# Wide elementwise operations moved from GpSimd to VectorE, and the routing and hand-over work of attention spread over its tiles, in a three-stage transformer block

## The chip, the cores and the metric

One core of one Trainium2 chip. The metric is device time in microseconds (us) of one execution.

## The reference

x is (4, 1024, 128) in float32: four batches of 1024 rows. Three stages are added onto x in turn.

```python
x = x + 0.5 * ffn(layernorm(x))        # pass 0
x = x + attn(layernorm(x))
x = x + 0.5 * ffn(layernorm(x))        # pass 1, same weights
# ffn(t): logits = t @ Wr.T + br; two best of 8 experts, softmax over the two
#   expert e: relu(t @ W1[e].T + b1[e]) @ W2[e].T + b2[e], hidden size 512
#   returns layernorm(t + weighted sum of the two) * gamma + beta
# attn(t): softmax(q1 k1^T) - lambda * softmax(q2 k2^T), times v, then an rms norm
```

## The kernel before

TensorE is PE, VectorE DVE, ScalarE ACT, GpSimd POOL, SyncE SP. A batch is 8 tiles of 128 rows (TB = 8, BATCHES = 4).

**The two passes.** For each batch the rows t are made by ACT (`make_rows`, L561), turned by PE (`turn_rows`), multiplied into logits (`logits`), and DVE picks the experts (`read_logits`, `choose`) and the place of each row (`place`), with an exponential by ACT (`gap`) and prefix sums by PE (`prefix`) between them. `copy_rows` makes the second copy of the rows and the one in `tgt`. POOL then writes each 128 rows with an indirect DMA to their expert's region in DRAM (`scatter`, L424, 16 pieces for a batch); `table` lists the tiles of the experts for a group of two batches. A pass is 78 slots, one tile of one expert each, 39 for a group. In a slot SP loads the rows (ring of 8), PE turns them (L842), multiplies with W1 (L850) and W2 (L860), ACT and DVE stage weights (L604, L1199) and take the results out of PSUM (L611, L1206, `add_b2` L1214). In pass 0 SP writes the results and POOL gathers them back (`gather`, L435); in pass 1 POOL sends each tile of results away with an indirect DMA (`send`, L446), and SP loads them when a group is through. Each `load` of SP in pass 1 also waits until the `send` of 8 slots earlier has landed, and loads of a group wait until all its rows are written (`group_ready`). Every engine's stream is one fixed order: the loops over slots `s` say in which slot a side job stands (STATS_AT = 1, TURN_AT = 9, CHOOSE_AT = 13, PLACED_AT = 20, GSLOTS = 39, LAST_AT = 45). POOL executes its stream in order, so a job behind a scatter waits for it.

**Merging.** The two results of a row are weighted and added to `tgt`, normalised (DVE statistics, POOL `rstd`: reciprocal root in L407 to L410; ACT `normalise`), multiplied with gamma, and added to x with beta. Before, POOL does the wide parts, each one instruction over a batch, 128 x 1024: `add_beta` (L416), `merge_add` (L462, L465), `add_tokens` (L470), `gain` (L476). Pass 0's batch 0 is merged in the slots of pass 0, batches 1 to 3 in attention, in tiles of the batch ahead. Pass 1 merges in its second half and in the tail after the last slot.

**Attention.** Query tile i of batch b: PE `scores` (L784 to L786) into banks 0 to 3, one pair for each softmax; DVE takes two maxima (L1374), ACT two exponentials (L667), DVE the difference (L1385) one tile later, PE turns the difference of two tiles earlier (`turn`, L910), ACT copies it (L641), and for each half batch PE multiplies with the values (`values`, L921, two pieces of 8 matmuls) and Wv. The next score pair of PE can start only when the exponential of the tile before has read its bank. The order around the change in the streams before: PE in tile i does `scores(i)`, then the extras, then `turn(i-2)`, and `values(b, 0, ·)` in tiles 6 and 7; DVE does the maxima of i, `difference(i-1)`, then the extras: `merge_tiles` in tiles 0 and 1, `add_values` and `x_stats(b-1)` in tile 4, `x_stats(b+1)` in tile 5. POOL in each batch does rstd, `merge_add`, `value_scale`, eight gathers or scatters, and only then the rstd of the two `x_stats`, which ACT's `make_rows` in tile 5 and `make_xn` in tile 6 wait for. At the end of a batch stand `logits`, `choose` and `place` of the batch before, and the hand-over to the next batch: `turn_xn`, `copy_xnT`, `xnT_rest`, `multiply_M`, `copy_xm`, `xm_rest`. `tgtT` lies in the memory of `sum_r`, which the merge of the next batch uses.

The lines that the text names are numbered as in the profile.

## Time and profile before

| | us |
|---|---|
| median of three runs | 785.39 (783.78 to 787.7) |
| the profiled execution, own time | 786.02 |
| its span | 784.3 |
| PE busy in the span | 588.6 (75%) |
| DVE busy | 518.8 (66%) |
| ACT busy | 413.5 (53%) |
| POOL busy | 384.9 (49%) |

The span runs from the first to the last instruction of the profiled execution; its own time has 1.7 us around it. Starts are us from the span's start. Start-up and first routing take the first 88 us, pass 0 then goes to about 251, attention to 549, pass 1 to 745, and the rest is the tail. Busy shares are means over these stages and say little by themselves.

### The profile page before, as it was taken

The page shows a single profiled execution, that of the slowest core. Times are in us where ns is not written, and L with a number is a line of the kernel's source. Part 1 is how long each engine was busy: PE and PEld are TensorE (multiplying, and loading weights), DVE is VectorE, ACT ScalarE, POOL GpSimd, SP SyncE. Part 2 cuts the span into 40 slices and gives each one's busy share as a digit, 9 for nine tenths or more (in the row PEclk, how much of TensorE's full clock was granted, in tenths as well). Part 3 has the DMA queues.
Part 4 walks back from the last instruction along what each step waited for, and adds up shares of the span by engine and source line. Part 5 has one row for each costly group of instructions (what it writes and reads, how often), then busy time and mean ns, then how long its engine had stood idle before and what let it go on. Part 6 is the DMA issues. An engine that isn't in the chain of part 4 may idle for free.

```text
span 784.3 us, 16226 instructions
## 1 busy us (share of the span) xinstructions
PE 588.6 (75%) x3864; PEld 508.4 (65%) x3864; DVE 518.8 (66%) x1630; ACT 413.5 (53%) x1103; POOL 384.9 (49%) x415
## 2 busy tenths in 40 slices
PE   2654599998998678976887667787989858788900
PEld 2544599998988555554655455653988747778900
DVE  4654666675786786994799476853648635888726
ACT  3443266655556377376647644653665434646621
POOL 6455055544453067168157313413556774666643
PEclk9955599999899999998999797998999988999965
DMA  8412244324331001001000001001122321412141
GB/s 281 123 56 62 54 106 109 93 69 111 95 93 52 1 10 41 3 12 34 11 28 21 8 7 49 24 4 47 40 65 72 97 62 47 152 54 59 45 161 54
DMA packets 53677, 49.18 MB, mean 63 GB/s; under 512 B 9863, under 2 KB 45875, under 8 KB 53073
## 3 DMA queue, kind: packets, MB, share of 16 engines
q1 hardware_dynamic: 44736, 31.25, 14.6%
q0 software_dynamic: 8640, 16.87, 7.0%
q8 instruction: 35, 0.57, 0.3%
q14 instruction: 58, 0.47, 0.2%
q10 hardware_dynamic: 208, 0.02, 0.0%
HBM read 25.99 MB, written 23.02 MB: 62 GB/s over the span
## 4 chain that ended last, share of the span: by engine, by line
PE 48%; DVE 20%; issue 11%; POOL 10%; ACT 6%; DMA 3%; DVEq 1%; ACTq 0%; POOLq 0%; SPq 0%
PE banks L850 15%; PE banks L860 14%; PE banks L921 5%; PE banks L828 3%; POOL zb L435 3%; ACT rowbuf L561 2%; PE banks L842 2%; PE banks L819 2%; POOL rs L408 2%; PE banks L784 2%; POOL rows L424 2%; PE banks L786 2%; PE banks L785 2%; DVE nb L1374 1%; DVE sum_r L1241 1%
## 5 line engine op out<-in xcount | busy, mean ns | idle before, releaser
L850 PE MATMUL banks<-scratch 128*128 128x128 f32 x1248 | 174.2, 284 | 19.4 <-DVE scratch L1199 16.8
L850 PEld LDWEIGHTS banks<-scratch 128*128 128x128 f32 x1248 | 157.7, 198 | 27.0 <-issue 20.5
L860 PE MATMUL banks<-blocks,scratch 128*128 x1248 | 169.1, 280 | 0.1
L860 PEld LDWEIGHTS banks<-blocks,scratch 128*128 128x128 f32 x1248 | 156.2, 197 | 0.7 <-issue 0.5
L1206 DVE TENSOR_SCALAR scratch<-banks,blocks 128x128 f32<-128x128 f32 x312 | 95.0, 345 | 65.7 <-PE banks L850 64.5
L424 POOL DMA_INDIRECT rows<-rowbuf,slot x96 | 95.6, 996 | 67.4 <-issue 37.7
L667 ACT ACTIVATE scratch<-banks,nb 128x1024 f32<-128x1024 f32 x64 | 71.1, 1114 | 81.0 <-DVE nb L1374 80.7
L611 ACT ACTIVATE scratch<-banks,blocks 128x128 f32<-128x128 f32 x312 | 97.7, 364 | 28.5 <-PE banks L850 27.6
L598 ACT ACTIVATE scratch<-banks 128x128 f32<-128x128 f32 x156 | 43.2, 277 | 128.7 <-PE banks L842 126.4
L1374 DVE TENSOR_REDUCE nb<-banks 128x1 f32<-128x1024 f32 x64 | 76.8, 1217 | 48.1 <-PE banks L786 47.0
L446 POOL DMA_INDIRECT results<-scratch x78 | 77.7, 996 | 61.0 <-DVE scratch L1214 43.0
L435 POOL DMA_INDIRECT zb<-yrows,slot x64 | 64.8, 1012 | 53.4 <-DVE scratch L1214 25.1
L784 PE MATMUL banks<-xnTh,xmh 128*128 128x512 f32 x128 | 59.8, 467 | 36.2 <-ACT scratch L667 29.8
L1199 DVE COPY scratch<-blocks 128x256 f32 x156 | 63.4, 407 | 27.3 <-PE banks L850 18.7
L1214 DVE TENSOR_TENSOR scratch<-banks,blocks 128x128 f32<-128x128 f32 x156 | 45.0, 289 | 32.6 <-PE banks L860 23.8
L921 PE MATMUL banks<-scratch,xn 128*128 128x512 f32 x128 | 62.6, 637 | 1.5 <-ACT scratch L641 1.5
L604 ACT ACTIVATE scratch<-blocks 128x256 f32 x156 | 63.7, 408 | 0.1
L842 PE MATMUL banks<-ident,scratch 128*128 128x128 f32 x156 | 43.9, 281 | 23.5 <-issue 12.2
L784 PEld LDWEIGHTS banks<-xnTh,xmh 128*128 128x128 f32 x128 | 26.3, 205 | 48.2 <-ACT scratch L667 33.9
L424 POOL DMA_INDIRECT rows<-scratch,slot x32 | 30.5, 953 | 51.9 <-DVE scratch L1214 51.9
L786 PE MATMUL banks<-xnTh,xml 128*128 128x512 f32 x128 | 54.2, 423 | 0.0
L785 PE MATMUL banks<-xnTl,xmh 128*128 128x512 f32 x128 | 53.9, 421 | 0.0
(175 smaller groups left out, 893.0 us busy)
## 6 DMA issues: line engine op xcount, KB each, us to landing
scratch<-rows SPq DMA_DIRECT2D x156, 64.5 KB
yrows<-scratch SPq DMA_DIRECT2D x78, 64.0 KB
scratch<-results SPq DMA_DIRECT2D x3, 1024.0 KB, 7.8
rows<-padrows SPq DMA_DIRECT2D x34, 64.5 KB
x<-in_L_attn_x_dram SPq DMA_DIRECT2D x4, 512.0 KB, 6.0
scratch<-in_L_ffn_W_dram SPq DMA_DIRECT2D x1, 2048.0 KB, 19.2
out_dram<-x SPq DMA_DIRECT2D x4, 512.0 KB, 6.1
rows<-rowbuf,slot POOLq DMA_INDIRECT x96
```

Source lines behind the costliest of these rows:

```text
L424: pool.indirect_dma_start(rows[b // GB], bass.IndirectOffsetOnAxis(slot_v[:, b, j, k:k + 1], 0), rows_of(p, b)[:, j, k, :], None).then_inc ...
L435: pool.indirect_dma_start(zb[:, i * D:(i + 1) * D], None, yrows[b // GB], bass.IndirectOffsetOnAxis(slot[:, b * PAIRS + i:b * PAIRS + i + ...
L446: pool.indirect_dma_start(results, bass.IndirectOffsetOnAxis(xt_v[:, r, D:ROW].bitcast(I32), 0), ys[:, r * D:(r + 1) * D], None, bounds_ch ...
L611: ins = act.activation(hT_of(T, c), hT_at(T, c), ACT.Relu, bias=blocks[:, B1_AT + c:][:, bass.ds(at, 1)], scale=1.0)
L667: act.activation(pp, banks[:, 2 * m * 512:(2 * m + 2) * 512], ACT.Exp, bias=nb[:, 2 * i + m:2 * i + m + 1], scale=1.0, accum_out=ll[:, i:i ...
L784: pe.matmul(o, ah, bh, start=True, stop=False)
L786: return pe.matmul(o, al, bh, start=False, stop=True)
L850: ins = pe.matmul(hT_at(T, c), staged(T, c), xT_of(T), start=True, stop=True)
L860: ins = pe.matmul(y_at(T), hT_of(T, c), blocks[:, W2_AT + c * D:][:, bass.ds(at, D)], start=(c == 0), stop=(c == FC - 1))
L921: ins = pe.matmul(bank(6), xn[b % 2][:, k * D:(k + 1) * D], dT[g][:, k * QG * P:(k + 1) * QG * P], start=(k == 0), stop=(k == TB - 1))
L1206: ins = dve.tensor_scalar(hT_of(T, c), hT_at(T, c), blocks[:, B1_AT + c:][:, bass.ds(at, 1)], 0.0, ALU.add, ALU.max)
L1374: dve.tensor_reduce(nb[:, c], banks[:, 2 * m * 512:(2 * m + 2) * 512], AX_X, ALU.max, negate=True).then_inc(nb_ready, 1)
```

## The change

It does the following.

- POOL's wide operations go to DVE, each in two halves of 128 x 512: beta of pass 0 in slots 18 to 25, beta of pass 1 in slots 31 to 38, the gain and the addition of the merge in attention's tile 5, tokens and gain of pass 1 in slots from LAST_AT + 5 and LAST_AT + 20 on and in the tail.
- In attention POOL does the rstd of both `x_stats` ahead of most gathers and scatters. The scatters of batch 0 stand in batches 2 and 3, those of batch 1 in batch 3; 8 of batch 2's stand ahead of the first send of pass 1, the other 8 one per slot in slots 0 to 7. Those of batch 3 are two per slot, in slots 20 to 27.
- `tgtT` gets a buffer of its own. The routing of batch b-2 (logits, choose, place) moves from the end of batch b-1 into tiles 1 to 3 of batch b (b = 2, 3); only that of batch 2 stays at the end of batch 3. `table(0)` moves into tile 4 of batch 3.
- `make_rows`, `make_xn` and the normalisation of the merge are done in halves in two tiles. `values(b, 0, 1)` and `turn(b, 5)` of PE go ahead of `scores(b, 7)`; `turn_xn` follows it. The waits for the split query matrix go into each score.
- DVE does `xnT_rest` in tile 7 and `xm_rest` ahead of the last difference, `add_values(b, 0)` in tile 0 of the next batch.

The core of the diff:

```diff
-        tgtT = sum_r
+        tgtT = sb("tgtT", S)
+        BETA_AT = 18
+        SENT_BEFORE = 8
+        def halves_of(tiles):
+            return range(tiles * TB // 2, (tiles + 1) * TB // 2)
+        def choose_tile(b):
+            return 1 if b == BATCHES - 1 else 2
...
 POOL, attention
-                if b > 1:
-                    scatter(1, b - 2, range(TB))
-                if b < BATCHES - 1:
-                    rstd(n)
-                    n += 1
-                    merge_add(b + 1)
-                if b:
-                    value_scale(b - 1, 1)
-                if b < 2:
-                    gather(b + 2, range(TB))
-                if b > 1:
-                    scatter(1, b - 2, range(TB, 2 * TB))
-                for _ in range((b > 0) + (b < BATCHES - 1)):
-                    rstd(n)
-                    n += 1
-                if b < 2:
-                    gather(b + 2, range(TB, 2 * TB))
+                last, after = b > 0, b < BATCHES - 1
+                if b == BATCHES - 1:
+                    scatter(1, b - 3, range(8, PAIRS))
+                if after:
+                    rstd(n)
+                    n += 1
+                if last:
+                    value_scale(b - 1, 1)
+                    rstd(n)
+                    n += 1
+                if after:
+                    if b < 2:
+                        gather(b + 2, range(4))
+                    rstd(n)
+                    n += 1
+                if b < 2:
+                    gather(b + 2, range(4, PAIRS))
+                if b == 2:
+                    scatter(1, b - 2, range(8))
+                if b == BATCHES - 1:
+                    scatter(1, b - 2)
                 value_scale(b, 0)
-            scatter(1, BATCHES - 2, range(6))
             value_scale(BATCHES - 1, 1)
+            scatter(1, BATCHES - 2, range(SENT_BEFORE))
             for s in range(SLOTS):
                 send(s)
-                if s % 2 and s < 20:
-                    i = 6 + s // 2
-                    scatter(1, BATCHES - 2, range(i, i + 1))
+                if s < PAIRS - SENT_BEFORE:
+                    scatter(1, BATCHES - 2, range(SENT_BEFORE + s, SENT_BEFORE + s + 1))
                 if s == STATS_AT + 3:
                     rstd(n)
-                if PLACED_AT <= s < PLACED_AT + 2 * TB:
-                    i = s - PLACED_AT
-                    scatter(1, BATCHES - 1, range(i, i + 1))
+                if PLACED_AT <= s < PLACED_AT + TB:
+                    i = 2 * (s - PLACED_AT)
+                    scatter(1, BATCHES - 1, range(i, i + 2))
...
 ACT, attention
+                    if last and i == (3 if after else 2):
+                        o_copy(b - 1, 1)
+                    if i == TB - 1:
+                        if after:
+                            make_xn(b + 1, n + after + last, halves_of(1))
+                        if not after:
+                            copy_tgtT(a, 0)
+                        dT_copy(b, i - 2)
+                        o_copy(b, 0)
+                    probabilities(i, 0)
+                    if after and i == TB - 1:
+                        copy_xnT(b + 1)
+                    probabilities(i, 1)
+                    if b > 1 and i == choose_tile(b) + 1:
+                        gap(a - 1)
+                    rows_tile = i - (5 if after else 4)
+                    if last and rows_tile in (0, 1):
+                        make_rows(1, b - 1, n + after, halves_of(rows_tile))
...
 PE, attention
+                    if i == TB - 1:
+                        turn(b, i - 2)
+                        values(b, 0, 1)
                     scores(b, i)
+                    if b > 1 and i == 1:
+                        logits(a - 1)
+                    if b > 1 and i == choose_tile(b) + 1:
+                        prefix(a - 1)
+                    if last and i == 1:
+                        values(b - 1, 1, 0)
+                        if not after:
+                            values(b - 1, 1, 1)
+                    if 2 <= i < TB - 1:
                         turn(b, i - 2)
                 if after:
                     turn_xn(b + 1)
+                    if last:
+                        turn_rows(a, 0)
                 multiply_Wv(b, 0)
                 if after:
+                    multiply_M(b + 1)
+                    if last:
+                        turn_rows(a, 1)
                 turn(b, TB - 2)
...
 DVE, attention
                     maxima(i)
+                    if after and i == TB - 1:
+                        xnT_rest(b + 1)
                     if i:
                         difference(i - 1)
+                    if last and i == 0:
+                        add_values(b - 1, 0)
+                    if b > 1 and i == 1:
+                        read_logits(a - 1)
+                    if b > 1 and i == choose_tile(b):
+                        at_once(choose(a - 1))
+                    if b > 1 and i == choose_tile(b) + 1:
+                        at_once(place(a - 1, b - 2))
+                    if b == BATCHES - 1 and i == 4:
+                        at_once(table(0))
                     if after and i == 5:
-                        dve.wait_ge(merged, b + 1)
+                        merge_add(b + 1)
                         x_stats(b + 1, n)
+                if after:
+                    xm_rest(b + 1)
                 difference(TB - 1)
...
 DVE, new
+            def add_beta(p, b):
+                dve.wait_ge(rows_ready, BATCHES * p + b + 1)
+                for q in range(2):
+                    xq = x[:, columns(b, q, 2)].rearrange("p (j d) -> p j d", d=D)
+                    ins = dve.tensor_tensor(xq, xq, betab[:, :].unsqueeze(1).broadcast_to([P, TB // 2, D]), ALU.add)
+                    if q:
+                        ins.then_inc(beta_added, 1)
+                    yield
+            def gain(r):
+                for q in range(2):
+                    rq = r[:, columns(0, q, 2)].rearrange("p (j d) -> p j d", d=D)
+                    steps.then(dve.tensor_tensor(rq, rq, gammab[:, :].unsqueeze(1).broadcast_to([P, TB // 2, D]), ALU.mult))
+                    yield
+            def merge_add(b):
+                dve.wait_ge(scaled, b)
+                at_once(gain(sum_r))
+                dve.wait_ge(beta_added, b + 1)
+                for q in range(2):
+                    c = columns(b, q, 2)
+                    ins = dve.tensor_tensor(x[:, c], x[:, c], sum_r[:, columns(0, q, 2)], ALU.add)
+                steps.then(ins)
```

## Rows read from the trace of the kernel before

**Rows 1.** Windows: length, busy us PE, PEld, DVE, ACT, POOL, clock; last: line L842 alone.
```profile
251.50:549.20 297.70, 227.79 (x990) 162.37 (x989) 211.97 (x513) 169.73 (x341) 124.27 (x133) 0.92 0.07 20
549.20:745.00 195.80, 163.49 (x1349) 157.11 (x1350) 127.74 (x424) 108.35 (x357) 126.41 (x124) 0.95 0.25 69
285.85:290.13 4.28, 3.97 (x22) 3.08 (x21) 4.06 (x7) 3.11 (x6) 3.81 (x3) 1.00 0.06 15
382.60:386.10 3.50, 3.27 (x19) 2.85 (x20) 3.12 (x14) 2.34 (x6) 1.54 (x3) 1.00 0.00 0
389.65:392.85 3.20, 2.97 (x18) 2.31 (x16) 2.79 (x15) 0.00 (x0) 0.00 (x0) 1.00 0.00 0
467.80:472.10 4.30, 0.00 (x0) 0.00 (x0) 3.89 (x17) 0.00 (x0) 2.72 (x3) 0.76 0.22 66
354.00:358.00 4.00, 4.00 (x13) 3.08 (x12) 3.85 (x18) 1.35 (x3) 3.39 (x3) 0.58 0.19 49
...
108.00:156.00 48.00, 7.09 (x26) 3.72 (x26) 1.00 0.41 104
```

**Rows 2.** Timeline of DVE: start, length, name, [idle before]; first maxima of tiles.
```profile
261.73 2.58 DVE L1374 TENSOR_REDUCE nb<-banks 128x1 f32<-128x1024 f32 x2 [1.80 <-PE banks L786]
...
318.62 2.52 DVE L1374 TENSOR_REDUCE nb<-banks 128x1 f32<-128x1024 f32 x2 [0.84 <-PE banks L786]
...
371.71 1.22 DVE L1374 TENSOR_REDUCE nb<-banks 128x1 f32<-128x1024 f32 x1 [10.52 <-PE banks L786]
...
392.86 2.35 DVE L1374 TENSOR_REDUCE nb<-banks 128x1 f32<-128x1024 f32 x2
...
446.65 1.23 DVE L1374 TENSOR_REDUCE nb<-banks 128x1 f32<-128x1024 f32 x1 [10.68 <-PE banks L786]
...
472.12 2.35 DVE L1374 TENSOR_REDUCE nb<-banks 128x1 f32<-128x1024 f32 x2
...
520.94 2.59 DVE L1374 TENSOR_REDUCE nb<-banks 128x1 f32<-128x1024 f32 x2 [6.43 <-PE banks L786]
```

**Rows 3.** Timeline of ACT: the rows of the router, batch 1 of attention.
```profile
361.62 3.18 ACT L561 ACTIVATE rowbuf<-x,nm,rs 128x128 f32<-128x128 f32 x8 [6.27 <-POOL nm L410]
```

**Rows 4.** Groups of instructions by line: busy us, mean ns of one.
```profile
L416 POOL TENSOR_TENSOR x<-x,betab 128x1024 f32<-128x1024 f32 x8 | 19.1, 2406 | 0.4 <-DVE scratch L1214 0.3
...
L1339 DVE TENSOR_TENSOR x<-x,scratch 128x512 f32<-128x512 f32 x4 | 2.7, 688 | 3.7 <-issue 2.9 <-POOL scratch L476 0.7
```

**Rows 5.** Two lines alone: duration ns min/median/max, first and last start.
```profile
L921 PE MATMUL banks<-scratch,xn x128: 590/592/1222, 296.4 to 545.2; 128*128 128x512 f32 x128
...
L1385 DVE SCALAR_TENSOR_TENSOR scratch<-scratch,cc x32: 1283/1285/3465, 270.1 to 525.7; 128x1024 f32<-128x1024 f32 x32
```

**Rows 6.** Timeline of POOL, pass 1 and its start.
```profile
549.24 0.19 POOL L454 TENSOR_SCALAR so<-ss 128x4 f32<-128x4 f32 x1 [2.77 <-ACT scratch L653]
...
567.45 0.20 POOL L410 TENSOR_SCALAR nm<-nm 128x8 f32<-128x8 f32 x1
...
604.38 0.98 POOL L446 DMA_INDIRECT results<-scratch  x1 [0.30 <-issue]
...
645.22 0.98 POOL L446 DMA_INDIRECT results<-scratch  x1 [0.30 <-issue]
...
745.68 1.45 POOL L446 DMA_INDIRECT results<-scratch  x1 [0.17 <-issue]
```

**Rows 7.** Timeline of DVE, second half of pass 1.
```profile
665.23 2.90 DVE L1199 COPY scratch<-blocks 128x256 f32 x1
...
694.38 3.42 DVE L1241 SCALAR_TENSOR_TENSOR sum_r<-zb,wts,sum_r 128x128 f32<-128x128 f32 x2
...
720.11 3.27 DVE L1241 SCALAR_TENSOR_TENSOR scratch<-scratch,wts 128x128 f32<-128x128 f32 x2
```

**Rows 8.** Timeline of ACT, pass 1: first weighing of results.
```profile
675.33 0.69 ACT L713 ACTIVATE sum_r<-zb,wts 128x128 f32<-128x128 f32 x2 [2.05 <-DMA zb<-results]
```

**Rows 9.** Timeline of DVE, the tail.
```profile
760.63 4.65 DVE L1241 SCALAR_TENSOR_TENSOR scratch<-scratch,wts 128x128 f32<-128x128 f32 x8 [13.58 <-POOL scratch L470]
```

186 lines of the change are left out of this document (80 added, 106 removed).

## The prediction

> **What bounds the kernel now.** I read the windows by stage first, then DVE's timeline of attention, then the waits of ACT and POOL in it, then pass 1. Attention takes 298 us of the span, with PE busy for 228 and DVE for 212 of them, pass 1 takes 196 [rows 1]. Neither engine is full in attention, so its time is made by tiles that wait. The maxima that open a tile date the batches: 56.9 us for batch 0, 74.2 for batch 1, 79.3 for batch 2, and 48.8 from batch 3's first tile to its last [rows 2]. A tile with nothing extra takes 4.28 us, of which DVE is busy for 4.06 and PE for 3.97 [rows 1]. So DVE's sum of work per tile is the floor, PE is just behind it. The large excess sits in two places. DVE stands 10.5 and 10.7 us idle in batches 1 and 2 before tile 7 [rows 2]: ACT was waiting for POOL's rstd [rows 3], which stands behind eight gathers or scatters. And 21.2 us (batch 1) and 25.5 us (batch 2) pass from tile 7 to the next batch's first tile [rows 2], with the routing and the hand-over in them. In pass 1 a slot can take 1.9 us (about 25 tiles turned in 48 us of pass 0 [rows 1]), but POOL is the queue to look at: a transfer is 0.98 us with 0.30 to the next, 1.27 on average, and from 604.4 to 645.2 one send and one scatter alternate without a pause [rows 6]. In the second half, DVE instructions of some 0.3 or 0.6 us take about 3 us while POOL has a wide operation [rows 7].
>
> **The change, part by part.** The sum is made against the profiled execution, 786.02 us, which is 0.6 above the median of the runs.
>
> Prices. One 128x1024 operation of POOL takes 2.4 us, DVE's half piece 0.69 [rows 4], so a pair costs 1.4 on DVE. Choosing takes 3.5, placing 3.2, the table 4.3 us of DVE [rows 1]. A statistics call on x is 2.3, adding values 1.15, half a merge 3.3, by my reading of the same timeline as rows 2.
>
> Pass 0: eight beta pieces in slots of 1.9 us in which DVE has about 0.6 free. I take 0.2 each, less 1.0 that POOL's four operations cost beside it: **+1** (bounds -1, and eight times 0.69, +5.5).
>
> Attention, as tiles of 4.3 us plus what DVE has extra, with PE's or ACT's wait where one ends later.
> Batch 0: tile 5 gains the merge's gain and sum on DVE, four pieces, +2.8. Tile 6 is the new weak place in every batch: turn(b,5) and the values' second half now stand ahead of scores(7), and turn(b,5) needs difference(5), which DVE makes at the end of tile 6. So: difference at +4.3, ACT's copy of the tile before at +4.7, turn 0.9, values 8 x 0.43 = 3.45, first score pair 1.4: tile 7 opens at +10.5. PE stands idle for some 4 us ahead of it, and after idle like that its clock was low: 0.58 of full between 354 and 358 [rows 1]. A matmul of values takes 592 ns at the median and 1222 at the slowest [rows 5]; I add 1.9. From tile 7 to the next batch's first tile: scores 1.4 after the opening, turn_xn 0.9, copy 1.0, xnT_rest 1.2, M 2.8, turn(6) 0.9, last difference 1.9 behind xm_rest: 11.1 together, where it was 17.2. Batch 0 becomes 60.3 (was 56.9).
> Batch 1: tiles 6.8, 7.9, 4.3, 5.1, 7.8, 9.1, then 12.4 and 12.0 (two turns of rows and a copy in the hand-over): 65.4 (was 74.2). Here rstd comes before the gathers, and the 10.5 goes.
> Batch 2: 6.8, 8.3, then choosing 8.0, placing 9.2 (it waits 1.7 for ACT's exponential, which stands behind squares), 7.8, 9.1, 24.4: 73.6 (was 79.3). The 25.5 us hand-over is gone, its routing has moved to the tiles.
> Batch 3 to its last tile: 4.0, 11.4 (both values halves and logits on PE), 9.4 (placing), 7.8, 8.6 (table), 4.3, 11.5: 57.0 (was 48.8).
> Sum 256.3 against 259.2: **-3**. The end of batch 3, whose routing stays, **-1**. Much is taken off, nearly as much is put back: 8 us of routing and table for batch 3, and three times the wait in tile 6. Bounds: -12 if the wait in tile 6 costs no clock and the small waits are covered, +18 if the low clock stays over the hand-over.
>
> Pass 1, first half. value_scale (549.2) is followed by eight scatters (10.2 us), then sends with a scatter each, and only behind the fifth pair comes the rstd that make_rows waits for. Eighteen transfers of 1.27 and 2.5 for the rstd end at 576.6, where they ended at 567.6 [rows 6]: +9 for all slots behind it. Then send 20 goes at 613.4 instead of 604.4, the eight slots with two scatters take 3.82 us each on POOL, and the last scatter ends at 644.0 instead of 645. The four sends left over until SP may load slot 39 take 5 us more. So PE resumes at 654.8 where it did at 650, but without the long idle and its low clock, 2.0: **+3**. Beside DVE's pieces a send takes 1.45 instead of 0.97 us [rows 6]; eight pieces stand in slots 31 to 38, two or three of them where POOL is the bound: **+1** (bounds 0 and 4). The Trainium skill, "SBUF — State Buffer", section "SBUF: two separate sides", says that while DVE runs a two-port operation GpSimd is locked out of their shared port pair and cannot write descriptors. By that rule every moved piece could stop a transfer, which speaks against this change; the trace agrees with 1.45 beside 0.97, which is about one piece's length and no more. If all eight counted, the sum would be 3 us higher.
>
> Pass 1, second half. Four beta operations stretched four slots from 1.9 to 3.55 us, 6 us together (one copy took 2.90 [rows 7]). That goes, but ACT waits for the first load of results anyway, 2.05 us already now [rows 8], and would stand there 5 us: -2. Tokens of two batches (3.42 where 0.6 is usual, with a stretch of low clock behind it [rows 7]) -6.3, the first gain (3.27) -2.6. DVE's own pieces, eight at 0.2: +1.6. Together **-9** (bounds -13 and -2).
>
> Tail. The last sends are no longer behind a gain: -1.5. Then DVE idles 13.6 us for ACT and POOL and makes a 4.65 us sum beside POOL's second token addition [rows 9]. Tokens on DVE take 1.4 instead of 2.4, the sum 2.5 instead of 4.65, the last gain 1.4 on DVE instead of 2.3 and a wait, against 2.8 for four token pieces that DVE did not have: -3.5. **-5** together (bounds -7, -2).
>
> Sum: +1 -3 -1 +3 +1 -9 -5 = -13: 786 - 13 = **773**.
>
> **The rivals.** (a) The early rows pay. If rstd of pass 1 costs the slots nothing, because scatters land and slots catch up, the last scatter ends 9 us sooner and the first half gives -6 instead of +4: 763. For it: POOL has 13 us of small idle times in this stage to take up the work. Against it: POOL's stream is in order and rstd stands where it stands.
> (b) DVE becomes the bound in the passes. If each of the 24 pieces in slots lengthens its slot by 0.7 instead of 0.2: +12, 785, no change. For it: DVE has two waiting instructions per slot on PE's path. Against it: slots with two 128x128 operations extra kept to about 2.0 us.
> (c) Slower: the low clock. It is the idle wait in tile 6 of batches 0 to 2. If the granted clock stays at half through values (+3.4), scores (+2.75) and M (+2.75) it costs 8.9 instead of 1.9 each, 21 more: 794. It decides where the clock stays below 0.7 from tile 6 to the next batch. Against it: in the stretch after the idle at 350 the clock was back at full within 5 us.
>
> **How the numbers follow.** A measurement tells 0.5% (4 us) from no change. The forecast gets 0.5, (a) 0.2, (b) 0.15, (c) 0.12, and 0.03 is for what I haven't seen. Faster: forecast and (a), with little of the forecast's own spread above 781: 0.71. Same: (b) and a bit: 0.16. Slower: 0.13. The forecast's own range is 765 to 780 by its bounds. For 8 in 10 it has to reach toward (a) and nearly to (b): 760 to 785; (c) stays out.
>
> **What would show it.** Right: in batches 1 and 2 no DVE idle of 10 us, but one of about 6 us before each tile 7, released by the scores and those by the values; first tiles 60, 65 and 74 us apart; make_rows of pass 1 starting some 9 us later after value_scale than now; no L1199 or L1241 of 3 us. Wrong: a tile 6 of under 8 us, hand-overs over 14 us, a slot 20 that isn't late, slots of over 2.2 us with beta in them.

## The result and the profile after

| | us |
|---|---|
| before, median of 4 runs beside the changed kernel | 786.51 (783.78 to 787.7) |
| changed, median of 4 runs | 773.24 (772.04 to 775.16) |
| ratio, 95% interval | 0.9838 (0.9808 to 0.9868) |
| the profiled execution, own time | 773.43 |
| its span | 771.7 |

The change gains 13 us, 1.6%. The forecast was 773, so the sum came out; the profile says which of its terms did.

First the stages of the changed kernel as windows: length, busy us (and instructions) of PE, PEld, DVE, ACT, POOL, granted clock, DMA share, GB/s. The four are attention to its last tile, its end up to the last value_scale, pass 1 up to send 38, and up to send 77.

```profile
258.00:515.25 257.25, 202.43 (x893) 145.57 (x893) 198.17 (x476) 156.44 (x307) 98.08 (x118) 0.93 0.07 19
515.25:544.10 28.85, 19.75 (x79) 13.18 (x77) 13.63 (x44) 10.50 (x29) 2.02 (x3) 0.76 0.07 19
544.10:657.10 113.00, 93.19 (x716) 88.35 (x717) 62.47 (x234) 55.33 (x179) 72.31 (x78) 0.91 0.24 65
657.10:738.00 80.90, 75.04 (x640) 72.08 (x638) 58.77 (x210) 53.06 (x178) 44.84 (x47) 1.00 0.27 82
```

In the last one PE is busy for 75.0 of 80.9 us at full clock: the second half of pass 1 is now bounded by PE's own slots, but for some 6 us. The first half is not; PE lost 20 us there, at a clock of 0.91.

The timeline of DVE, first maxima of tiles (start, length, name, idle before and what ended it), against [rows 2]:

```profile
258.01 2.60 DVE L1419 TENSOR_REDUCE nb<-banks 128x1 f32<-128x1024 f32 x2
...
309.68 1.23 DVE L1419 TENSOR_REDUCE nb<-banks 128x1 f32<-128x1024 f32 x1 [9.14 <-PE banks L780]
...
320.48 2.35 DVE L1419 TENSOR_REDUCE nb<-banks 128x1 f32<-128x1024 f32 x2
...
372.30 1.22 DVE L1419 TENSOR_REDUCE nb<-banks 128x1 f32<-128x1024 f32 x1 [6.54 <-PE banks L780]
...
384.24 2.59 DVE L1419 TENSOR_REDUCE nb<-banks 128x1 f32<-128x1024 f32 x2 [1.06 <-PE banks L780]
...
444.09 2.60 DVE L1419 TENSOR_REDUCE nb<-banks 128x1 f32<-128x1024 f32 x2 [7.89 <-PE banks L780]
...
456.05 2.59 DVE L1419 TENSOR_REDUCE nb<-banks 128x1 f32<-128x1024 f32 x2 [1.07 <-PE banks L780]
...
515.25 2.59 DVE L1419 TENSOR_REDUCE nb<-banks 128x1 f32<-128x1024 f32 x2 [7.52 <-PE banks L780]
```

The first tiles are 62.5, 63.8 and 71.8 us apart and batch 3 goes 59.2 to its last tile, 257.2 in all, where 259.2 stood before. The idle times of 10.5 and 10.7 us in batches 1 and 2, which ACT's wait for POOL made, are gone, and one of 6.5 to 9.1 us stands before each tile 7 in their place, ended by the scores. The hand-overs (tile 7 to the next first tile) take 10.8, 11.9 and 12.0 us.

The timeline of POOL through pass 1: value_scale, the end of the rstd, send 20, the last scatter, send 38 and the last send, against [rows 6]:

```profile
544.11 0.19 POOL L460 TENSOR_SCALAR so<-ss 128x4 f32<-128x4 f32 x1 [21.36 <-ACT scratch L631]
...
572.48 0.20 POOL L422 TENSOR_SCALAR nm<-nm 128x8 f32<-128x8 f32 x1
...
609.81 0.97 POOL L452 DMA_INDIRECT results<-scratch  x1 [0.62 <-issue]
...
639.35 0.96 POOL L430 DMA_INDIRECT rows<-rowbuf,slot  x1 [0.30 <-issue]
...
657.07 0.97 POOL L452 DMA_INDIRECT results<-scratch  x1 [0.93 <-DVE scratch L1225]
...
738.06 0.97 POOL L452 DMA_INDIRECT results<-scratch  x1 [0.30 <-issue]
```

Counted from value_scale, the rstd ends at +28.4 (before +18.2), send 20 goes at +65.7 (before +55.1), the last scatter at +95.2, send 38 at +113.0 (before +108.0), the last send at +193.9 (before +199.5, at 748.70 us). The tail from there to the end takes 33.6 us, before 35.6. Part of the +65.7 is particular to this profile: in six others whose POOL does the same up to there, send 20 goes at +63.8 to +64.1.

So between the two profiled spans, 784.3 and 771.7: start-up +0.1, pass 0 from the first to the last tile turned -1.9 (157.3 to 155.4), from there to the first maxima -1.9 (16.1 to 14.3), attention -2.0, its end +0.6, pass 1 to send 38 +4.9, to send 77 -10.4, tail -2.0: -12.6.

### The profile page after: what moved, and what is told of

The parts are those of the page before. It is cut to its first block, busy times and chain, and to the rows that moved or that the text cites. A ratio compares the mean times of both kernels' runs of the same rounds, so it can differ in the third digit from the quotient of the medians.

```text
span 771.7 us, 16264 instructions
## 1 busy us (share of the span) xinstructions
PE 591.1 (77%) x3864; PEld 511.0 (66%) x3864; DVE 517.2 (67%) x1672; ACT 413.9 (54%) x1103; POOL 333.6 (43%) x394
## 4 chain that ended last, share of the span: by engine, by line
PE 51%; DVE 25%; issue 8%; ACT 7%; POOL 4%; DMA 3%; DVEq 0%; ACTq 0%; SPq 0%; POOLq 0%
PE banks L845 16%; PE banks L855 14%; DVE nb L1419 5%; PE banks L922 5%; PE banks L822 3%; PE banks L778 2%; PE banks L779 2%; PE banks L780 2%; POOL rows L430 2%; PE banks L837 2%; DVE st_x L1072 2%; DVE scratch L1430 2%; PE banks L813 2%; PE banks L911 1%; DVE mv L1078 1%
## 5 line engine op out<-in xcount | busy, mean ns | idle before, releaser
L845 PEld LDWEIGHTS banks<-scratch 128*128 128x128 f32 x1248 | 158.3, 199 | 17.3 <-issue 12.6
L589 ACT ACTIVATE scratch<-banks,blocks 128x128 f32<-128x128 f32 x312 | 97.4, 363 | 20.0 <-PE banks L845 18.9
L1419 DVE TENSOR_REDUCE nb<-banks 128x1 f32<-128x1024 f32 x64 | 76.4, 1215 | 46.7 <-PE banks L780 45.1
L778 PE MATMUL banks<-xnTh,xmh 128*128 128x512 f32 x128 | 58.7, 459 | 33.8 <-ACT scratch L645 33.7
L1210 DVE COPY scratch<-blocks 128x256 f32 x156 | 47.4, 304 | 25.1 <-PE banks L845 15.3
L419 POOL TENSOR_SCALAR rs<-mv 128x8 f32<-128x8 f32 x20 | 5.3, 267 | 126.6 <-DVE mv L1078 126.0
## 6 DMA issues: line engine op xcount, KB each, us to landing
scratch<-in_L_ffn_W_dram SPq DMA_DIRECT2D x1, 2048.0 KB, 19.6
```

The source lines that it names most:

```text
L589: ins = act.activation(hT_of(T, c), hT_at(T, c), ACT.Relu, bias=blocks[:, B1_AT + c:][:, bass.ds(at, 1)], scale=1.0)
L778: pe.matmul(o, ah, bh, start=True, stop=False)
L845: ins = pe.matmul(hT_at(T, c), staged(T, c), xT_of(T), start=True, stop=True)
L1419: dve.tensor_reduce(nb[:, c], banks[:, 2 * m * 512:(2 * m + 2) * 512], AX_X, ALU.max, negate=True).then_inc(nb_ready, 1)
```

## The experiments

Twelve kernels ran, in four sittings, each beside runs of the kernel before, whose medians were 786.76, 785.37, 786.59 and 786.11. The ratios below go to those. Each kernel has one profile, and stages vary between profiles of kernels with the same code in them: the start-up, whose end (first tile turned) lies between 88.2 and 91.0 us; pass 0, 154.7 to 156.6 us in nine profiles; attention, 254.3 to 258.3 us in seven; send 38 to send 77, 80.0 to 82.8 us in nine; the tail, 32.6 to 33.6 us in nine. A difference inside these bounds is not told by one profile.

### The wide operations alone

```diff
 kernel before; POOL
-                    add_beta(0, s - 2 * PAIRS)
-                    add_beta(1, s - GSLOTS - 1)
-                    add_tokens((s - LAST_AT) // 4 - 1)
-                    gain((s - LAST_AT - 19) // 10)
 and DVE's pieces at the slots of the changed kernel
+                if BETA_AT <= s < BETA_AT + 2 * BATCHES:
+                    next(first_betas)
```

> The kernel before with only the wide operations of the two passes on VectorE: beta in halves in both passes, tokens and gain. Attention, its merge, the order of the transfers, the last rows one per tile stay as they were. Theory 1 (the wide operations are nearly the whole gain): pass 0 -1.9 us (the stretched slots near 160 us), second half of pass 1 -10.8, tail -2, as the two traces differ: about 771, ratio 0.981. The prediction's own terms (+1 -9 -5) give 773. Rival (the spread attention work carries about half): 778 to 780, and slots of pass 1 above 39 still late.

776.03 us, ratio 0.9885 (0.9852 to 0.9919): -10.7. The same three points of POOL's timeline, value_scale, send 38, send 77:

```profile
548.71 0.19 POOL L450 TENSOR_SCALAR so<-ss 128x4 f32<-128x4 f32 x1 [2.11 <-ACT scratch L627]
...
658.65 0.97 POOL L442 DMA_INDIRECT results<-scratch  x1 [2.06 <-DVE scratch L1188]
...
739.89 0.97 POOL L442 DMA_INDIRECT results<-scratch  x1 [0.30 <-issue]
```

Send 38 to send 77 takes 81.2 us, as in the changed kernel (81.0) and not as before (91.4 by rows of the same kind). The tail is 32.7. Attention is as it was (261 us, with the 11 us waits before tile 7). So the gain of the second half of pass 1 and of the tail comes with the wide operations alone. The total fell 5 us short of theory 1. Of these, 3.7 can be named: the first half went from 108.0 to 109.9 and attention happened to be 1.8 longer.

### The wide operations put back

```diff
 changed kernel; the reverse of the edit above
+                    add_beta(0, s - 2 * PAIRS)
+                    add_beta(1, s - GSLOTS - 1)
+                    add_tokens((s - LAST_AT) // 4 - 1)
+                    gain((s - LAST_AT - 19) // 10)
```

> The changed kernel with beta, tokens and gain back on GpSimd, where the kernel before has them; attention's merge on VectorE, the spread routing and the order of the transfers stay as changed. Theory 1: entry to attention -1.8, attention -2, its end +0.6, first half of pass 1 +5: about 787.5, so nothing is left of the gain. Rival (attention carries half): 779 to 780. The stretched slots near 160 us and the 3 us VectorE operations in pass 1 are back in both.

785.37 us over 10 runs, ratio 0.998 (0.995 to 1.0009): no difference from the kernel before can be told. The two halves add up within the noise, -10.7 and -1.4 against -13.3 for the whole. Attention's side, with its merge on DVE, the spread routing and the new order of transfers, shows no gain by itself. The reason is in its own stages: -1.7 at the entry and -1.6 in attention by this profile (257.6 for 259.2), and +2.9 to send 38 (656.84 - 545.91 = 110.9 against 108.0).

### Beta alone put back

```diff
 changed kernel; POOL
+                    add_beta(0, s - 2 * PAIRS)
+                    add_beta(1, s - GSLOTS - 1)
```

> The changed kernel with beta alone back on GpSimd (slots 32 to 35 of pass 0, 40 to 43 of pass 1); tokens and gain stay on VectorE. Theory (beta's price was in the slots it stretched, and only part of it returns because ACT waits for the results' load): +1.5 in pass 0 and +3 in pass 1, 777 to 778. Rival (tokens and gain carry all of the 12 us between the changed kernel and the one with all wide operations back): 773 to 775.

775.28 us, ratio 0.9857 (0.9815 to 0.99), 2 above the changed kernel's 773.24, within what can be told. That is also the edge of the rival, so the total does not decide between them. The profile shows where beta costs: send 38 to send 77 takes 84.8 us (656.06 to 740.82) instead of 81.0, outside the 80.0 to 82.8 of the same code. Pass 0, 156.3 instead of 155.4, is inside its bounds. The tail is 33.8, where it is 36.9 with tokens and gain back too. Between send 38 and send 77 that kernel takes 89.8, so beta has about 4 us of this stretch and tokens and gain about 5, and the tail is theirs alone. By the medians tokens and gain have the larger part, 785.37 - 775.28 = 10.1 us, and beta 2.0.

### The rstd of pass 1 ahead of the scatters

```diff
 changed kernel; POOL
-        SENT_BEFORE = 8
+        SENT_BEFORE = 0
-            scatter(1, BATCHES - 2, range(SENT_BEFORE))
             for s in range(SLOTS):
                 send(s)
-                if s < PAIRS - SENT_BEFORE:
-                    scatter(1, BATCHES - 2, range(SENT_BEFORE + s, SENT_BEFORE + s + 1))
                 if s == STATS_AT + 3:
                     rstd(n)
+                if STATS_AT + 3 <= s < STATS_AT + 3 + PAIRS:
+                    i = s - STATS_AT - 3
+                    scatter(1, BATCHES - 2, range(i, i + 1))
```

> The changed kernel with the 16 scatters of batch 2 moved behind the rstd of pass 1, one beside each send from slot 4 on (8 stood ahead of the first send, and one each in slots 0 to 7). Nothing is left out. Theory (the late rstd starves the slots for some 10 us of GpSimd's time that is never caught up, as the 16 us of small idle times between 583 and 608 us show): send 20 about 10 us sooner after value_scale (56 instead of 65.7), send 37 about 103 to 105 instead of 111, total 765 to 768. Rival (a) of the prediction (rstd costs the slots nothing, transfers alone set slot 39): no change, 773.

766.25 us over 6 runs, ratio 0.9753 (0.9727 to 0.9778): 7 us below the changed kernel, as the theory had it. Windows of the same 20 us in both, the changed kernel's and this one's (columns as above):

```profile
564.00:584.00 20.00, 13.19 (x85) 13.00 (x85) 5.45 (x18) 8.85 (x27) 15.04 (x17) 0.70 0.25 64
```

```profile
564.00:584.00 20.00, 17.83 (x158) 17.41 (x157) 10.65 (x37) 15.22 (x44) 15.03 (x16) 1.00 0.28 71
```

POOL is as busy in both (15.0 us); it only does other things first. With the scatters ahead, PE makes 85 matmuls at a clock of 0.70, with the rstd ahead 158 at full clock. POOL's timeline here (value_scale, send 20, the last scatter, send 38):

```profile
544.92 0.19 POOL L460 TENSOR_SCALAR so<-ss 128x4 f32<-128x4 f32 x1 [21.35 <-ACT scratch L631]
...
604.58 0.99 POOL L452 DMA_INDIRECT results<-scratch  x1 [0.30 <-issue]
...
633.94 0.96 POOL L430 DMA_INDIRECT rows<-rowbuf,slot  x1 [0.30 <-issue]
...
651.74 0.98 POOL L452 DMA_INDIRECT results<-scratch  x1 [0.92 <-DVE scratch L1225]
```

The last scatter goes at +89.0 instead of +95.2, send 38 at +106.8 instead of +113.0. Send 20 went at +59.7, later than the 56 expected, since 16 scatters now stand beside sends 4 to 19. Rival (a) of the prediction, that a late rstd costs the slots nothing, is out.

### Six scatters back in GpSimd's idle time

The kernel before has six of batch 2's scatters ahead of the last value_scale. The changed kernel has all of them behind it, and its POOL stands idle for 21.4 us there (the first row of its POOL timeline above).

```diff
 changed kernel; POOL
+            scatter(1, BATCHES - 2, range(6))
             value_scale(BATCHES - 1, 1)
-            scatter(1, BATCHES - 2, range(SENT_BEFORE))
+            scatter(1, BATCHES - 2, range(6, SENT_BEFORE))
```

> The changed kernel with 6 of batch 2's scatters ahead of the last value_scale, as the kernel before has them, and 2 behind it. The rows' places are there at 532 us, value_scale goes at 544.1 after 21.4 us of GpSimd's idle time. Theory (the change moved six transfers out of that idle time to behind value_scale, where they delay rstd and slots; this, not the order of rstd alone, is the first half's +4.9): rstd ends near 21 us after value_scale instead of 28.4, send 38 near 106 to 107 instead of 113.0, total 766 to 768. Rival (value_scale itself waits behind them, or the slots are then bound by something else): value_scale 2 to 5 us later after tile 7, total 771 to 773.

766.78 us over 6 runs, ratio 0.9763 (0.9737 to 0.979): 6.5 below the changed kernel. POOL's timeline: the first of the six, value_scale, the end of the rstd, send 38.

```profile
532.33 1.07 POOL L430 DMA_INDIRECT rows<-rowbuf,slot  x1 [10.39 <-DVE slot L1146]
...
543.30 0.19 POOL L460 TENSOR_SCALAR so<-ss 128x4 f32<-128x4 f32 x1 [2.71 <-ACT scratch L632]
...
565.40 0.20 POOL L422 TENSOR_SCALAR nm<-nm 128x8 f32<-128x8 f32 x1
...
649.68 0.97 POOL L452 DMA_INDIRECT results<-scratch  x1 [0.93 <-DVE scratch L1226]
```

value_scale is not late: tile 7 to value_scale takes 28.9 us as in the changed kernel, since ACT's squares end it, and POOL still waits 2.7 us for them. The rstd ends at +22.1, send 38 goes at +106.4, where the changed kernel has +113.0 and the kernel before +108.0. So by these profiles the first half's +4.9 is +6.6 for six transfers that lost their cover and -1.6 for everything else that changed up to there; the 1.6 us by which the changed kernel's profile is late at send 20 are in the +6.6. The medians, which do not hang on one profile, give 6.5.

### The last rows one per slot

```diff
 changed kernel; POOL
-                if PLACED_AT <= s < PLACED_AT + TB:
-                    i = 2 * (s - PLACED_AT)
-                    scatter(1, BATCHES - 1, range(i, i + 2))
+                if PLACED_AT <= s < PLACED_AT + PAIRS:
+                    i = s - PLACED_AT
+                    scatter(1, BATCHES - 1, range(i, i + 1))
```

> The changed kernel with the last batch's 16 scatters one per slot (slots 20 to 35) as before, where the change has two per slot. Theory (GpSimd's transfers set when slot 39 can be loaded; two per slot put the last scatter ahead of the sends that slot 39 does not need): last scatter ends near 106 us after value_scale instead of 96.2, send 37 near 115 instead of 111.1, total +4 to +5: 777 to 778. Rival (the same number of transfers, so the same time; the loads of slots 28 to 38 are late by as much with two per slot): 773, send 37 at 111.

779.75 us over 10 runs, ratio 0.9927 (0.99 to 0.9955): 6.5 above the changed kernel. The windows show what two per slot avoids:

```profile
640.00:650.00 10.00, 0.46 (x5) 0.27 (x3) 1.38 (x5) 0.00 (x0) 7.56 (x8) 0.69 0.12 36
650.00:660.00 10.00, 7.03 (x43) 6.79 (x44) 3.32 (x10) 3.05 (x11) 0.97 (x1) 0.63 0.17 41
```

PE stands idle for 12.5 us before it turns the tile of slot 39, as in the kernel before (12.2 us), and its granted clock is 0.63 in the window in which it comes back. In the changed kernel it has no such idle time there. The last scatter goes at +104.2, send 37 at +115.2 against +111.1. POOL's transfers are as many; but the sends of slots 32 to 35, which the load of slot 39 does not need, no longer stand ahead of the last scatters. So the part "two per slot" is worth 6.5 us. It pays for the late rstd and hides it.

### The first scores waiting for all four pieces

```diff
 changed kernel; PE
+                pe.wait_ge(xmh_sb, 4 * b + 4)
+                pe.wait_ge(xml_sb, 4 * b + 4)
                 for i in range(TB):
 scores()
-                        if i == 0:
-                            pe.wait_ge(xmh_sb, 4 * b + 2 * m + h + 1)
-                            pe.wait_ge(xml_sb, 4 * b + 2 * m + h + 1)
```

> The changed kernel with the first scores of each batch waiting for all four pieces of the multiplied keys, as before, where the change waits per piece. Theory (this wait, which the prediction left out, is the 1.7 us by which attention's entry got shorter, 16.1 to 14.4, and is worth about as much at each hand-over): entry 16.1, hand-overs 12.5 to 14 instead of 10.8 to 12, total +5 to +6: 779. Rival (in the hand-overs DVE's last difference comes behind the same pieces anyway): entry 16.1 alone, +1.7: 775.

778.16 us over 7 runs, ratio 0.9903 (0.9871 to 0.9935), 5 above the changed kernel. By its profile the rival is right on the mechanism: the entry takes 16.1 us again, and the hand-overs 10.9, 12.0 and 12.0, as in the changed kernel. That is 1.9 us against its 14.3. The profiled execution, 780.33, is 6.9 above that of the changed kernel. The other 5 are not where the edit stands: the first tile is turned 2.3 us later (90.7 for 88.4), pass 0 is 0.7 and attention 1.7 longer. The first two are within what these stages vary; attention, 258.9, is 0.6 above it, and its granted clock is 0.92 where the changed kernel has 0.93. So the stage shows 1.9 us for the edit. The medians lie 4.9 apart, more than chance explains (the ratios' intervals do not overlap), and the 3 us between the two stay open.

### The scores of tile 7 first

```diff
 changed kernel; PE, batches 0 to 2 (ACT's copies behind the exponentials in the same way)
-                    if i == TB - 1:
+                    if i == TB - 1 and not after:
                         turn(b, i - 2)
                         values(b, 0, 1)
                     scores(b, i)
+                    if i == TB - 1 and after:
+                        turn(b, i - 2)
+                        values(b, 0, 1)
```

> The changed kernel with TensorE's tile 7 of batches 0 to 2 in the old order: scores(7) ahead of turn(5) and the second half of the values, ACT's copies behind the exponentials. Theory of the prediction (the wait for difference(5) and the values is paid in tile 6 and the low clock comes with it): tile 6 falls from 13.2, 10.6 and 11.9 us to about 8, hand-over grows from 11 to 12 us to 15 (turn and values stand ahead of the turn of the next batch), about -1.5 us per batch: 769. Rival (the values only change places, the hand-over grows by all that tile 6 loses or more): 773 to 777.

768.66 us over 6 runs, ratio 0.9806 (0.9769 to 0.9842). The runs lie at 767.3 to 768.8 (four) and at 772.9 and 775.3, and the interval overlaps that of the changed kernel, so by itself this is inconclusive. In the profile tile 6 falls to 5.1 us in batch 0 and 4.2 in batch 1, and the hand-over grows to 15.6 and 19.6: 20.8 and 23.7 together, against 24.0 and 22.5 in the changed kernel. In batch 2 it is 4.2 and 18.9, 23.0 together against 23.9.

### Both mends together, with batch 3, and with six scatters ahead

Three kernels. The first has the edits of "The rstd of pass 1 ahead of the scatters" and "The scores of tile 7 first":

```diff
-        SENT_BEFORE = 8
+        SENT_BEFORE = 0
-                    if i == TB - 1:
+                    if i == TB - 1 and not after:
```

> The changed kernel with both mends: scatters of batch 2 behind the rstd of pass 1, and scores(7) of batches 0 to 2 ahead of turn(5) and the values. Nothing is left out. If they add up (-7.0 and -2 to -4): 761 to 764, ratio to the kernel before near 0.970. Rival (the second one was chance, its runs lay in two groups around 768 and 774): 766.

763.00 us over 6 runs (760.37 to 766.61), ratio 0.9718 (0.9683 to 0.9753). That is 10.2 below the changed kernel and 22.4 below the kernel before in the same sitting. It is 3.3 below the early rstd alone. The two ratios' intervals overlap, but the profiles point the same way: attention takes 252.2, 252.6 and 253.3 us in the three kernels with the reordered tile 7 of batches 0 to 2, and 254.3 to 258.3 in the seven with the change's order. So it is worth about 3 us. The timeline of DVE, tile 7 of batch 0 and the first tile of batch 1:

```profile
300.82 1.23 DVE L1424 TENSOR_REDUCE nb<-banks 128x1 f32<-128x1024 f32 x1 [0.98 <-PE banks L782]
...
316.60 2.35 DVE L1424 TENSOR_REDUCE nb<-banks 128x1 f32<-128x1024 f32 x2
```

Tile 6 takes 5.0 us, the hand-over 15.8. In batches 1 and 2 all that left tile 6 stands in the hand-over: both together take 23.6 and 23.9 us, for 22.5 and 24.0 with the early rstd alone. What remains as a gain is in batch 0, 20.8 for 23.1 at nearly the same granted clock (0.92 and 0.93). Why only batch 0 gains is not shown.

In the change's order the length of tile 6 goes with the clock. Here are the three tiles 6 of batches 0, 1 and 2 in the changed kernel (windows, columns as above):

```profile
296.52:309.68 13.16, 9.09 (x25) 5.28 (x24) 3.95 (x7) 7.82 (x15) 10.32 (x12) 0.74 0.12 31
361.75:372.30 10.55, 6.69 (x25) 3.77 (x24) 3.94 (x8) 9.24 (x19) 8.33 (x10) 1.00 0.12 32
432.18:444.09 11.91, 8.04 (x25) 4.85 (x24) 3.95 (x7) 9.36 (x19) 8.95 (x11) 0.86 0.09 29
```

PE makes 25 matmuls in each. In batch 0 the granted clock is down to 0.50, the level of 1.2 GHz, for part of the tile, in batch 2 for a shorter part, and in batch 1 not at all. The eight profiles with this order have 24 such tiles, and all of them fall into line: at a mean granted clock of 1.00 a tile 6 takes 10.5 to 10.6 us (5 tiles), at 0.86 it takes 11.9 to 12.2 (12 tiles), at 0.74 or 0.75 it takes 13.1 to 13.5 (7 tiles).

The second lets batch 3 follow the same order:

```diff
-                    if i == TB - 1 and not after:
-                        turn(b, i - 2)
-                        values(b, 0, 1)
                     scores(b, i)
-                    if i == TB - 1 and after:
+                    if i == TB - 1:
                         turn(b, i - 2)
                         values(b, 0, 1)
```

> The kernel with both mends, and scores(7) ahead of turn(5) and the values in batch 3 too. Nothing is left out. Theory (tile 6 of batch 3 waits as the others did): its tile 6 falls from 12 to 13 us to 6, and from tile 7 to the last value_scale it takes 32 to 33 us instead of 28.9, together -2 to -3: 760 to 761. Rival (at the end of attention nothing waits for scores(7) but the same chain, values and squares included): no change, 763.

763.62 us over 6 runs (758.63 to 768.65), ratio 0.9695 (0.9657 to 0.9732): the same as without it. In its profile, which is of its slowest execution, tile 6 of batch 3 fell to 8.2 us where 6 was expected, and from tile 7 to value_scale 32.1 us pass instead of 27 to 29. The ratio points one way and the median the other, so this stays at no difference that can be told.

The third adds the six scatters ahead of value_scale to the first:

```diff
+            scatter(1, BATCHES - 2, range(6))
             value_scale(BATCHES - 1, 1)
...
-                if STATS_AT + 3 <= s < STATS_AT + 3 + PAIRS:
-                    i = s - STATS_AT - 3
+                if STATS_AT + 3 <= s < STATS_AT + 3 + PAIRS - 6:
+                    i = s - STATS_AT - 3 + 6
```

> The kernel with both mends (763.0), and 6 of batch 2's scatters ahead of the last value_scale, the other 10 one per slot from slot 4 on. Theory (up to slot 39 GpSimd's queue is the bound, and six transfers less behind value_scale are 7.6 us less of it): last scatter near 82 us after value_scale instead of 89, send 38 near 100 instead of 106.9, total 756 to 758. Rival (with the rstd early the slots are near TensorE's own rate): 761 to 763.

759.68 us over 6 runs (758.02 to 761.42), ratio 0.9665 (0.964 to 0.969): the fastest kernel here, 3.4% below the one before. The last scatter goes at +83.6, send 38 at +101.5 (642.08 - 540.60) instead of +106.9. Six transfers less brought 5.4 us at send 38 and 3.3 in the total, of the 7.6 that they take. The early rstd and the six scatters ahead overlap: either alone is worth 6.5 to 7, and both bring the rstd nearer to value_scale. Together POOL's queue is less often the bound: in the windows of 20 us from 560 to 600 PE is already busy for 17.8 and 18.3 us.

```profile
560.00:580.00 20.00, 17.80 (x158) 17.36 (x157) 10.78 (x38) 14.92 (x44) 15.43 (x16) 1.00 0.28 71
580.00:600.00 20.00, 18.26 (x156) 17.34 (x155) 16.49 (x67) 10.96 (x37) 13.65 (x15) 1.00 0.31 80
600.00:620.00 20.00, 14.62 (x115) 13.02 (x114) 9.49 (x36) 7.79 (x27) 15.12 (x17) 1.00 0.32 84
```

In the third window the three transfers per slot still hold it.

### Beta made twice

```diff
 changed kernel; DVE, add_beta
+                    spare = tgtT[:, columns(0, q, 2)].rearrange("p (j d) -> p j d", d=D)
+                    dve.tensor_tensor(spare, xq, betab[:, :].unsqueeze(1).broadcast_to([P, TB // 2, D]), ALU.add)
                     ins = dve.tensor_tensor(xq, xq, betab[:, :].unsqueeze(1).broadcast_to([P, TB // 2, D]), ALU.add)
```

> The changed kernel with each of the 16 beta pieces made twice on VectorE, once more into an unused tile; the output stays as it is. It adds 16 operations of 128x512, some 11 us of VectorE, in slots 18 to 25 of pass 0 and 31 to 38 of pass 1. Theory (a piece in a slot costs little, since the slots are set by other things): the prediction's 0.2 each gives +3, what the trace of the changed kernel shows in pass 0 (TensorE 8.00 of 8 us busy) gives 0 to +1: 773 to 776. Rival (b) of the prediction (each piece lengthens its slot by its 0.7): +11, 784.

776.73 us, ratio 0.9862 (0.9817 to 0.9907), 3.5 above the changed kernel's median: about 0.2 for each of the 16 pieces on the mean, and far from 11. They do not all cost the same: by the profile pass 0 takes 159.3 us instead of 155.4, about 0.5 for each of its 8 pieces, and pass 1 up to send 38 takes 112.8 instead of 113.0. And it is not DVE that lengthens the slot. The timeline of POOL in pass 0, first in the changed kernel, then with two pieces per slot:

```profile
130.83 0.96 POOL L430 DMA_INDIRECT rows<-scratch,slot  x1 [1.16 <-DVE scratch L1225]
132.73 0.96 POOL L430 DMA_INDIRECT rows<-scratch,slot  x1 [0.94 <-DVE scratch L1225]
```

```profile
134.34 1.81 POOL L430 DMA_INDIRECT rows<-scratch,slot  x1 [0.31 <-issue]
136.46 1.82 POOL L430 DMA_INDIRECT rows<-scratch,slot  x1 [0.30 <-issue]
```

and the pieces of DVE beside them, in the same order:

```profile
131.03 0.68 DVE L1265 TENSOR_TENSOR x<-x,betab 128x512 f32<-128x512 f32 x1
...
132.93 0.68 DVE L1265 TENSOR_TENSOR x<-x,betab 128x512 f32<-128x512 f32 x1
```

```profile
134.04 0.68 DVE L1266 TENSOR_TENSOR tgtT<-x,betab 128x512 f32<-128x512 f32 x1
134.64 0.69 DVE L1267 TENSOR_TENSOR x<-x,betab 128x512 f32<-128x512 f32 x1
...
136.16 0.69 DVE L1266 TENSOR_TENSOR tgtT<-x,betab 128x512 f32<-128x512 f32 x1
```

With one piece, the transfer starts 0.20 us before the piece and takes its usual 0.96. With two, the transfer starts 0.30 us after the first piece's start and as much before the second's, and ends 0.8 us after the second is over, after 1.81. A transfer and the gap of 0.30 then fill 2.12 us, and that is the distance of the slots (134.04 to 136.16), where it was 1.90. So POOL's queue became the bound in these slots. That is 1.8 us of pass 0's 3.9; the rest is not placed.

One piece ahead of a transfer holds it too. In the changed kernel's second half of pass 1 a last addition of the merge starts 0.04 us before a send:

```profile
718.48 0.67 DVE L1384 TENSOR_TENSOR x<-x,sum_r 128x512 f32<-128x512 f32 x1
718.52 1.48 POOL L452 DMA_INDIRECT results<-scratch  x1 [0.60 <-issue]
```

The send ends 0.85 us after the addition. Eight transfers of this profile start inside a 128x512 operation of DVE whose two inputs both lie in SBUF. They take 0.96 to 1.48 us, and each ends 0.84 to 0.89 us after that operation does. Maxima that DVE takes from PSUM (L1419) leave a transfer at 0.94 to 1.06 us, whichever starts first.

## Why the prediction was right, and where it wasn't

**The total** was 773.0 against a measured 773.24, from a sum of -13 against spans 12.6 apart. The terms:

| term | predicted | profiles |
|---|---|---|
| pass 0 | +1 | -1.9 |
| entry to attention | not priced | -1.9 |
| attention to its last tile | -3 | -2.0 |
| end of batch 3 | -1 | +0.6 |
| pass 1 to send 38 | +4 | +4.9 |
| second half of pass 1 | -9 | -10.4 |
| tail | -5 | -2.0 |

The two last rows are cut differently by the prediction: its tail has -1.5 for the last sends, which stood behind a gain of POOL (743.13 to 745.51 us). They lie before send 77, so like for like it is -10.5 for -10.4 and -3.5 for -2.0.

Right by their mechanism and nearly by size are attention, the first half and the second half.

**Attention.** The first tiles came 62.5, 63.8 and 71.8 us apart for 60.3, 65.4 and 73.6, and batch 3 took 59.2 for 57.0. Tile 6 was the new weak place as named: 13.2, 10.6 and 11.9 for 12.4, hand-overs 10.8, 11.9 and 12.0 for 11.1, 12.0 and 12.0. The terms written for the hand-over of batch 0 add up to 10.1, not 11.1; the measured 10.8 lies between. For tile 6 both parts of the price can be told apart: the 10.5 us without the clock are what a tile 6 takes at full clock, and the flat 1.9 us for the low clock stand for 0, 1.4 to 1.7, or 2.5 to 3.0, by how much of the tile it covers. That the place is a cost was true to about 3 us only, as the reordered kernels show: values and turn have to be done before the next batch's matrix in any order, so most of what tile 6 waited for, the hand-over would.

The clock also explains most of why the same attention code takes 254.3 us in one kernel and 257.2 in another. Batch 0 in the changed kernel and in the one with the early rstd:

```profile
258.01:320.48 62.47, 47.45 (x201) 34.50 (x200) 47.58 (x99) 36.55 (x69) 22.30 (x25) 0.89 0.07 17
```

```profile
261.71:321.08 59.37, 45.67 (x201) 33.08 (x200) 47.67 (x100) 36.31 (x69) 23.52 (x25) 0.94 0.06 18
```

Batches 1, 2 and 3 agree to 0.2 us in these two. In the eight profiles with this order batch 0 takes 62.5 us at 0.89, 60.9 at 0.92 and 59.4 to 59.6 at 0.94. What makes the clock fall in one and not in the other is not shown.

**First half of pass 1.** rstd +10.2 for +9, send 20 +10.6 for +9 (+8.6 to +9.0 in six other profiles), and the last scatter ends at +96.2, before +95.7. PE turns the tile of slot 39 at +107.5 for the +105.6 of the prediction, before +100.3, with no long idle time ahead of it, and by send 38 it has won back 2.3 of the 7.2 for the 2.0 that were put on the clock. The experiments separate what the prediction had in one term. Eighteen transfers stand ahead of the rstd's end, as counted, but six of them had stood in POOL's idle time before, and putting them back there gives 6.5 us; the rstd ahead of the scatters gives 7; two scatters per slot are worth 6.5 the other way. The +4 was right as a difference, and the step "+9 for all slots behind it" was a cost that had a cheap cure in the kernel before. The descriptors' +1 did not come: the eight sends of slots 31 to 38 take 0.97 or 0.98 us, and of the transfers beside the pieces only one scatter took more, 1.09. So the other parts cost 4.9 us for the +3 that they had.

**Second half of pass 1.** -10.4 for -9. PE is busy for 75.0 of 80.9 us, and no copy or second result of 3 us is left. Beta has 4 us of it, where the prediction had 2: it let ACT's wait for the results eat 4 of the 6 us. Two sends stand behind idle times of POOL of 3.62 and 2.34 us there now; send 46 to send 47 takes 4.6 us, where it takes 1.9 with beta on POOL, so 2.7 were eaten. Tokens and gain have 5 of it, where 8.9 were predicted. The sum is closer than its parts.

**The terms that failed.** Pass 0 was put at +1, "0.2 each, less 1.0 that POOL's four operations cost beside it". No cost of the pieces shows: in the 12 us from 156, where POOL's beta stood before, PE is busy for 12.00 instead of 11.51 us, and the slots with pieces are 1.90 us apart. Two profiles put the whole of pass 0 at -1.9 (the changed kernel) and -2.3 (wide operations alone), against 157.3 before; but with all of them back it took 155.6, and the same code varies by 2 us, so the part that POOL's beta had in them stays open. The entry to attention, where the scores' waits per piece let tile 0 open before all four are made, was in the diff and had no term: 1.9 us, shown by the kernel that undid it. The tail was overestimated, -2.0 for -3.5 like for like, or -3.3 against the kernel with the wide operations back (36.9). Along its chain the sum of 4.65 us takes 2.56, as predicted, and the wait for the first tokens is 0.9 shorter. The second batch's token pieces add 1.4. The gain with its wait gives 1.5, and from the last addition to the end it takes 0.9 longer than before, which had no term. Against the terms as written, pass 0, the entry and the tail were off by 2.9, 1.9 and 3.0 us with both signs and mostly cancelled. So the mechanisms of the large terms were right, and that the total came within 0.3 us is luck.

**The rivals.** (a) is out: bringing the rstd forward gives 7 us in one way and 6.5 in another, so its delay cost something. (b), 0.7 for each piece, is out: the slots with pieces are 1.90 us apart, and doubled pieces cost 0.2 each on the mean and 0.5 in pass 0. (c), the low clock over the whole hand-over, did not come: in batch 0 the clock was 0.93 from 306.0 to 309.5 us, just before tile 7, and 1.00 behind it.

The Trainium skill, "SBUF — State Buffer", section "SBUF: two separate sides", says that DVE and GpSimd lock a shared port pair, that GpSimd cannot write descriptors while a DVE operation holds it, and that whichever starts first has the pair for the whole instruction while the other waits. With two pieces the trace agrees: the transfers end 0.8 us after the second piece. With one piece behind the transfer's start it agrees that the transfer stays at 0.96 us; but the piece inside it takes its usual 0.68 us, so no wait of DVE shows. So the moved pieces cost by whether a transfer starts inside them: the order of start inside the slot decided.

## What to carry to other kernels

When an in-order queue carries both bulk transfers and a small operation that another engine's next step waits for, put the transfers where the queue idles anyway and the small operation ahead of the rest; here six scatters moved out of an idle time of 21 us, or thirteen ahead of one rstd, are worth 6.5 to 7 us that the next stage could not catch up. Price the opposite effects of a reordering separately: only the parts show that one of them can be had alone. A wide operation moved off GpSimd pays by what it did to VectorE's instructions beside it and by when its result was due, and one half-width piece per slot showed no cost as long as no transfer began inside it.

## What the runs showed of the hardware that was not expected

A GpSimd indirect transfer of 128 rows takes 0.96 us when VectorE's 128x512 addition starts after it. When it starts inside such an addition it ends some 0.85 us after the addition does: 1.48 us with one that started 0.04 us ahead, 1.82 us with two, of which the second started while the transfer ran. VectorE's maxima out of PSUM do not hold it. At nearly equal POOL load, the order of its instructions alone moved PE's granted clock over 20 us from 0.70 to 1.00; PE made 85 matmuls in the one and 158 in the other. In tile 6, with a wait of PE in all three batches, the mean granted clock was 0.74, 1.00 and 0.86, and the 24 tiles of this kind in eight profiles take 10.5 to 10.6 us at 1.00, 11.9 to 12.2 at 0.86 and 13.1 to 13.5 at 0.74 or 0.75.
